# Bias product of the first half of the heads: one piece of sixteen per axis behind the value product, instead of two pieces of eight around it

## The reference

```python
attn = jnp.einsum('bqc,bkc->bqk', q * scale, k)
r_q = q.reshape(-1, WS, WS, HD)
rel_h = jnp.einsum('bhwc,hkc->bhwk', r_q, Rh)
rel_w = jnp.einsum('bhwc,wkc->bhwk', r_q, Rw)
attn = (attn.reshape(-1, WS, WS, WS, WS) + rel_h[:, :, :, :, None] + rel_w[:, :, :, None, :]).reshape(-1, N, N)
attn = jax.nn.softmax(attn, axis=-1)
out = jnp.einsum('bqk,bkc->bqc', attn, v)
```

## Time and profile before

| | |
|---|---|
| median of 3 runs | 715.27 us (713.39 to 717.22) |
| profiled execution, its own time | 715.34 us |
| span in the profile | 713.6 us |
| PE busy | 642.6 us (90%) |
| PEld busy | 492.6 us (69%) |
| DVE busy | 359.8 us (50%) |
| ACT busy | 338.1 us (47%) |
| POOL busy | 112.8 us (16%) |
| mean granted clock of PE | 0.979 |

### The profile page before, as it was taken

One profiled execution on the slowest core, in us unless ns is written; L12 is line 12 of the kernel. 1 busy time (PEld: TensorE's weight loads), 2 busy tenths in 40 slices (PEclk: granted clock), 3 DMA queues, 4 the chain that ended last, 5 costly groups with the idle time before them and its releaser, 6 DMA issues.

```text
span 713.6 us, 14706 instructions
## 1 busy us (share of the span) xinstructions
PE 642.6 (90%) x5696; PEld 492.6 (69%) x5696; DVE 359.8 (50%) x982; ACT 338.1 (47%) x807; POOL 112.8 (16%) x156
## 2 busy tenths in 40 slices
PE   2889998999899989999999999999999977899996
PEld 2577757875787678767776777677767753676764
DVE  4466336633663466344734473547344713166665
ACT  3346543654365426542664266426642641254463
POOL 1500040004000400040004000400010021023130
PEclk9999999999999999999999999999999975999999
DMA  4673820085008400740073006300640000000000
GB/s 99 150 182 99 194 83 1 10 196 135 1 5 199 123 2 3 193 97 2 3 166 90 1 4 160 96 0 4 157 100 1 3 1 1 0 1 24 23 23 22
DMA packets 32954, 47.31 MB, mean 66 GB/s; under 512 B 5468, under 2 KB 13982, under 8 KB 32886
## 3 DMA queue, kind: packets, MB, share of 16 engines
q1 hardware_dynamic: 31654, 45.98, 26.5%
q10 hardware_dynamic: 1232, 0.40, 0.2%
HBM read 7.05 MB, written 1.57 MB: 12 GB/s over the span
## 4 chain that ended last, share of the span: by engine, by line
issue 58%; PE 22%; POOL 11%; DVE 5%; DMA 2%; ACT 2%; POOLq 0%; SPq 0%; ACTq 0%; DVEq 0%
PE bank L544 3%; POOL xn L735 3%; POOL q_nat L722 3%; PE bank L696 2%; PE bank L366 2%; POOL rstd L715 2%; PE bank L554 2%; PE bank L690 2%; PE bank L474 2%; PE bank L493 2%; POOL x_all L728 2%; PE bank L681 1%; PE bank L444 1%; PE bank L672 1%; DVE neg_max L877 1%
## 5 line engine op out<-in xcount | busy, mean ns | idle before, releaser
L1117 ACT ACTIVATE PT<-bank 98x392 f32<-98x392 f32 (+1 forms) x288 | 137.2, 491 | 152.0 <-PE bank L474 147.6
L877 DVE TENSOR_REDUCE neg_max<-bank 98x2 f32<-98x392 f32 x192 | 104.9, 561 | 111.7 <-PE bank L444 111.2
L474 PE MATMUL bank<-q_aug,k_aug 127*98 127x196 f32 (+1 forms) x672 | 112.5, 263 | 3.4 <-DMA q_aug<-negT 1.3
L444 PE MATMUL bank<-k_aug,q_aug 126*98 126x196 f32 x384 | 88.8, 317 | 9.8 <-DVE neg_max L877 9.0
L474 PEld LDWEIGHTS bank<-q_aug,k_aug 127*98 127x98 f32 (+1 forms) x672 | 87.5, 168 | 13.8 <-ACT PT L1117 8.1
L544 PE MATMUL bank<-yT,w_up 96*128 96x512 f32 x192 | 87.1, 611 | 1.0 <-ACT yT L1143 1.0
L722 POOL TENSOR_TENSOR q_nat<-st_q 96x392 f32<-96x392 f32 (+2 forms) x48 | 24.9, 546 | 357.1 <-DVE st_q L845 357.1
L554 PE MATMUL bank<-w_down,PT 128*128 128x192 f32 x384 | 76.8, 331 | 3.7 <-ACT PT L1148 3.7
L366 PE MATMUL bank<-xT,w_qkv 97*96 97x256 f32 (+2 forms) x272 | 76.3, 397 | 1.8 <-ACT xT L1054 1.4
L444 PEld LDWEIGHTS bank<-k_aug,q_aug 126*98 126x98 f32 x384 | 56.1, 167 | 25.0 <-DVE neg_max L877 16.0
L544 PEld LDWEIGHTS bank<-yT,w_up 96*128 96x128 f32 x192 | 37.4, 196 | 45.7 <-issue 44.2
(11 more groups left out here) (88 smaller groups left out, 864.3 us busy)
## 6 DMA issues: line engine op xcount, KB each, us to landing
q_aug<-st_q SPq DMA_DIRECT2D x64, 192.0 KB
k_aug<-st_k SPq DMA_DIRECT2D x64, 192.0 KB, 4.5
q_aug<-st_r SPq DMA_DIRECT2D x64, 168.0 KB
x_all<-in_x SPq DMA_DIRECT2D x4, 384.0 KB, 7.2
q_aug<-negT ACTq DMA_DIRECT2D x96, 1.5 KB
k_aug<-st_p SPq DMA_DIRECT2D x16, 74.2 KB, 2.3
w_up<-in_up_w SPq DMA_DIRECT2D x2, 576.0 KB
w_down<-in_down_w SPq DMA_DIRECT2D x4, 288.0 KB
```

Of the source, the lines that this page charges most:

```text
L444: last = t_.matmul(b[0:HALF, WIN * r:WIN * r + WIN], q_aug[0:NEG, h, c + HALF * r:c + HALF * r + HALF], k_aug[0:NEG, h, c:c + WIN], start= ...
L474: last = t_.matmul(b[0:keys, m * k:m * k + m], k_aug[0:NEG + 1, h, c + keys * k:c + keys * k + keys], q_aug[0:NEG + 1, h, c:c + m], start= ...
L877: ins = v.tensor_reduce(neg_max[0:HALF, slot(n, u), e:e + 5:4], b[0:HALF, 0:2 * WIN] .rearrange("p (r m) -> p r m", r=2), AX.X, ALU.max, n ...
L1117: s.activation(PT[0:rows, i % 8, 0:m], bank[2 + i % 2][0:rows, 0:m], ACT.Exp).then_inc(S["exp"], 1)
```

## The change

In steps 5 and 6 the bias product of an axis was issued in two pieces of eight products, one behind the pieces of e = 0 and one behind those of e = 3. It is now one piece of sixteen at e = 2. The line stands below the value product of e = 2 in the code, so on PE it comes right behind that.

```diff
-                            if u in (5, 6) and e in (0, 3):
-                                bias(n + 1, 0, u - 5, 8 * (e // 3), 8 * (e // 3) + 8)
+                            if u in (5, 6) and e == 2:
+                                bias(n + 1, 0, u - 5, 0, HH)
```

## The result

The changed kernel takes 719.5 us (median of 8 runs, 718.61 to 723.92), the kernel before 714.77 us in the 8 runs beside it (711.5 to 717.35). The ratio is 1.0077, with a 95% interval of 1.0046 to 1.0108: slower by 5.5 us. All eight executions lie in the forecast range. The profiled execution took 718.79 us, its span is 717.0 us.

The account below looks back on a forecast made before the run. PE was taken to bound steps 5 to 7 by a thin margin, with ACT right behind. Six jobs losing 1.04 us and job 3 losing 0.49 sum to 6.7 us on 715.34: 722.0 us, range 717.5 to 724.5.

Parts of the forecast that it names:

- The price of the pieces: PE, steps 5 and 6: value and joined bias products together take 1.40 us in each step.
- The drain rule: Changing the tiling mode drains the array; four changes per axis go away, saving the value product's whole idle time.
- The lower bound: All idle time saved, sixteen products at their loads' span: value plus bias 1.11 and 1.19 us; 3.2 us lost, 718.5.
- (5,2): Step 5, PE: scores wait for the row maximum of (5,0), a new wait of 0.27 us.
- (5,3): Step 5: scores at 212.43, exponential at 213.12 us where it was 212.72, late by 0.40.
- (6,1) and (6,2): Step 6: PE waits 0.4 us for exponential (5,3), then 0.6 us for exponential (6,0).
- (6,3) and (7,2): scores_T (6,3) at 216.35, before 215.31, behind the whole bias product; ACT's chain then makes (7,2) 1.04 us late.
- Job 3: Padding product between (6,3) and (7,0) gives ACT 0.55 us of slack, so only 0.49 of 1.04 is lost.
- Faster: Rival: only PE's work counts, 0.26 to 0.42 us saved per axis, 711.7 to 709.4 us; chance 0.05.
- made up behind step 7: No-change rival: later waits absorb half the shift, 718.6 us, or nearly all, 715.5 to 717; chance 0.15.
- The clock did not fall: Much slower rival: PE's new gaps halve the clock from (6,1) to (7,2), 24 us more, 746; chance 0.03.
- The line that the prediction drew for slower: Slower means above 718.8 us, as a measurement tells about 0.5% (3.6 us) from no change; slower got 0.79.

Follow-up runs that it names:

- the late runs above: Changed kernel with ACT's copy_rt, or copy_rt and copy_o, moved behind the next exponential: 720.5 and 712.7 us; kernel before with both moved: 711.63 us.
- The two runs of one step each: Kernel before with one piece of sixteen at e = 2 in step 5 alone, 714.46 us, or in step 6 alone, 715.67 us; before beside them 716.15.
- the same late copies: ACT's copies behind the next exponential, job 3's axis w copy_rt kept behind (6,3); ratio to before 0.9973 in two pieces, 0.9951 in the changed order.

## Why the prediction was right, by its own steps

The prediction named 722.0 us and +6.7 us; the median is 719.5 us, the turns sum to +6.4 us, and the ratio gives +5.5 us.

**The price of the pieces.** The bias product started 214.56 - 213.87 = 0.69 us behind the value product in step 5 and 218.41 - 217.77 = 0.64 in step 6, where the next piece started after 0.80 and 0.76 before. The prediction gave back half of PEld's idle time, 0.65 and 0.66; measured are 0.69 and 0.64, so 0.11 and 0.12 us given back where 0.15 and 0.10 were put. The drain rule of the Trainium skill ("TensorEngine Tiling (Array Packing)", "Key Properties") agrees with the sign; of the whole idle time of 0.31 and 0.19 us, which it would have saved, the trace shows 0.11 and 0.12. From the bias product to the next piece it was 0.70 in both steps, against 0.75 taken from the end of the job. Together 1.39 and 1.34 us, where the prediction had 1.40 twice. In step 5 that is in part luck: the value product's share came out 0.04 larger and the bias product's 0.05 smaller. The lower bound has a slip: the earlier trace rows give 1.34 / 2 = 0.67 us for the loads of sixteen products, 0.08 less than 0.75 and not 0.13, so the lowest price would have given 719.3 us instead of 718.5.

**(5,2).** A wait for the row maximum of 0.27 was forecast, PEld shows 0.22.

**(5,3).** Late by 0.40 forecast, 0.38 measured (exponential at 215.94 - 212.67 behind (5,0), before 212.72 - 209.82).

**(6,1) and (6,2).** Waits of about 0.4 and 0.6 were forecast, counted by starts. `scores_T` (6,1) stands 216.47 - 212.22 = 4.25 us behind that of (5,0), where 4.26 was forecast. (6,2) stands 0.95 behind (6,1), before 0.35: 0.60 of waiting, as forecast. (PE's idle times of 0.35 and 0.42 are shorter than that, since they begin where a product is taken to end.) `scores_T` (6,2) stands 217.42 - 212.22 = 5.20 us behind that of (5,0), before 4.82: late by 0.38, where 0.40 was forecast.

**(6,3) and (7,2).** `scores_T` (6,3) stands at 219.11, 6.89 us behind (5,0), before 5.93: late by 0.96 against 1.04. (7,2) stands at 221.07, 8.85 behind (5,0), before 7.89: 0.96 too. That stays: in job 2 the exponentials are 0.95 late at (7,3), in all of step 8 and in the turn. All six turns lie between 0.93 and 1.00. The 0.08 that is missing is the 0.06 of the second pair of pieces and the 0.02 at (5,3).

**Job 3.** Forecast 0.49, measured 0.59 to 0.63. The slack on ACT was as read: exponential (6,3) is 0.98 late and (7,0) 0.41. But another wait, which the prediction did not have, takes some of that slack away again. PE's transposes behind (7,0) wait for the `copy_rt` of axis w, as in the late runs above, and not for ACT's exponentials:

```profile
293.37 0.64 PE L400 MATMUL bank<-ident,rt 128*84 128x128 f32 x4 [0.29 <-ACT rt L1084]
```

Exponential (7,1) is 0.84 late and (7,3) 0.63. Before, the same transposes did not wait. So the forecast 0.49 came near 0.59 with one term missing.

**The split.** The prediction put 0.40 on step 5 and 0.64 on step 6. The two runs of one step each show 0.38 and 0.57, and they add up.

**What decides.** The prediction said that the half at e = 0 fills the time in which ACT catches up, and that from (6,3) to (7,2) ACT's chain decides. The second is shown, by moving ACT's copies alone. The first was given more weight than it has: with the whole piece at e = 3 the same place is bare, PE waits in it, and only 0.13 is lost.

**The rivals.** Faster did not come. Value and bias products together do take less of PE's time in one piece, but no pair of runs shows it in a turn: with the same late copies the kernel in two pieces gains more in every turn but job 3's. The loss was not made up behind step 7. The clock did not fall in the turns, where it is 1.00.

**The size of the whole.** The forecast of 722.0 is 2.5 us above the median of 719.5. Of that, 0.3 lies in the turns (6.7 against 6.4) and 0.6 in the base (715.34 against a median of 714.77). The other 1.7 us is not in the turns. The prediction had no term for how the time at half clock differs between executions, at the start and at the end of job 7; by the spans above this moves single executions of one kernel by as much as the change itself. It is enough to part the 4.7 us between the medians, the 5.5 of the ratio and the 6.4 of the turns, but no run shows that it does. That the median came as near as 2.5 us is in part luck; the mechanism rests on the turns and on the order of the lateness within them. The line that the prediction drew for slower, 718.8 us, was passed by 0.7 us only; that the kernel is slower rests on the interval of the ratio, which stays above 1, and on the turns.

## What to carry to other kernels

In a pipeline of two buffers between PE and another engine, look for the instruction that starts the other engine's longest chain, here the product ahead of an exponential with two copies behind it. Filler for PE belongs behind that instruction, not ahead of it, and copies that nothing waits for belong behind the next link of the chain. Where whole executions scatter, compare the distance between the same instruction in two rounds of the loop, and check the one round whose buffers rotate differently.

## What was not expected of the hardware

In job 7 and behind it, with the same instructions, the granted clock stood at 0.50 for 24 us in one kernel's profiled execution and for 10 us in the other's, and the part from exponential (5,0) of job 7 to the end differed by 3.9 us. In both the clock is at 1.00 again behind it, but for the last 5 us. At the start the time at half clock differs as much, from none to 27 us in the twelve traces. The runs do not show what sets the length.
